# Twelve upper weight pieces and twelve value clips given to GpSimd in a quantised attention and expert kernel

## The chip, the core and the metric

The kernel runs on one core of a Trainium2 chip. The core has a matrix engine (TensorE, PE in the rows), VectorE (DVE), ScalarE (ACT), GpSimd (POOL), and a queue engine for transfers (SyncE, SP). They run side by side and wait for each other through semaphores. The metric is the device time of one launch in microseconds (us), as the median of several runs; less is better.

## The reference

A small vision block on 32 images of 36 tokens (1152 tokens, 192 features each):

```
h = patches @ proj_w.T + proj_b                       # 1152 x 768 -> 192
q, k, v = fq(layernorm(h)) @ fq(ww1).T                # 12 heads of 64
a = softmax(fq(q) @ fq(k).T / 8)                      # within one image
h = h + fq(fq(a) @ fq(v)) @ fq(ww2).T + bb2
n = layernorm(h); e = argmax(n @ Wg + bg)             # one of 4 experts per token
h = h + gelu(n @ W1[e] + b1[e]) @ W2[e] + b2[e]       # 192 -> 768 -> 192
```

fq(x) is s * (clip(round(x / s) + z, 0, 15) - z). The kernel keeps fq's integers: one instruction scales and rounds to int16, a second one clips to [-z, 15 - z] and writes bfloat16. "Clip" below means that second instruction, a maximum and a minimum from int16 to bfloat16.

## The kernel before, in words

Each engine has its own program, written out by hand; nothing is reordered later, so an instruction that waits holds up all that stands behind it on its engine.

The work has four stretches. First nine tiles of 128 tokens are embedded and normalised. Then come 15 steps, one for each pair of images (`for i in range(STEPS)` in every engine's program), in which four chunks of eight images are taken through the linear maps, the scores, the softmax and the product with the values, as a pipeline over the engines. After them the last tiles are normalised, the gate picks an expert for every token, and the tokens' rows are scattered to memory by expert. Last, twelve tiles of 128 slots go through the experts.

In a step, TensorE makes the scores of the next pair (L1151), the linear maps that are due (L1126 for the values, L1130 for queries and keys), the transposed probabilities (L1169) and the product with the values (L1186). ScalarE rounds the linear maps from PSUM to int16 (`vint` at L504 for the values, `kint` L510, `qint` L513), takes the exponential (L528), copies the transposed probabilities (L550) and rounds the outputs (L537). VectorE takes the maximum of each row of scores (L754), subtracts it (L760), sums the exponentials (L865), takes the reciprocal (L869), multiplies (L873) and clips (all clips are at L682, by the helper `clip`: `aq` probabilities, `q`, `k`, `v`, `oT` outputs). In some steps it also finishes a tile of tokens: the residual (L890), its moments (L692, L696), the variance plus epsilon (`veps`, L700) and, a step later, the normalised tile (`xn`, L905). Between the last two GpSimd takes the power -1/2 (`rstd`, L430, the helper `scale`). It also makes the low half of four tiles (L449).

Values come in groups of 768 columns, one for each pair of images: the tile `v` has seven buffers, `vint` two. `lin_groups(i)` says which groups step i holds; values of chunks 1 to 3 are due in steps 2, 3, 6, 7, 10 and 11, two in each. ScalarE makes `vint` in that step, VectorE clips it one step later.

The experts' float32 weights are brought in 16 pieces (`SPLITS`): eight of W1 with 768 columns, eight of W2 with 576. Each is split in two float16 parts: the upper part is the weight times 64, rounded to float16 (`split_high`, ScalarE L522), the lower part is what is left (`split_low`, VectorE L749, four in the steps and twelve behind the routing). `splits_at(i)` puts the eight upper parts of W1 into steps 1 to 8 and four of W2 into steps 11 and 12, at the end of a step of ScalarE; the last four come behind the steps.

GpSimd's program between the embedding and the scatter was nine short instructions, each of which waits for VectorE or ScalarE.

Of the kernel before, what the change touches and what calls it, by code (L numbers as in the profile page):

```python
# [11 lines left out]
ALU = mybir.AluOpType  # L12
# [10 lines left out]
WSCALE = 64.0  # L23
# [6 lines left out]
def vit_kernel(nc, patches_d, proj_w_d, proj_b_d, quant_d, ww1_d, ww2_d, bb2_d,  # L30
# [13 lines left out]
    _, NEXP, HM = b1_d.shape  # L44
# [23 lines left out]
    with ExitStack() as ctx:  # L68
# [3 lines left out]
        def sem(name):  # L72
            return ctx.enter_context(nc.semaphore(name))
# [126 lines left out]
        def xs(j):  # L200
# [35 lines left out]
        aT_ps, aT_ok, o_ps, o_int, o_ok = map(sem, ("aT_ps", "aT_ok", "o_ps", "o_int", "o_ok"))  # L236
        pr_ps, h2_ok, xn_ok, xhi_ok, xlo_ok, xnT_ps, xnT_ok, gate_ps = map(sem, (
            "pr_ps", "h2_ok", "xn_ok", "xhi_ok", "xlo_ok", "xnT_ps", "xnT_ok", "gate_ps"))
        pool_lo_ok = sem("pool_lo_ok")
        whi_ok, wlo_ok, route, onehot_ok, count_ps, logit_ok, slot_ok, slot_row_ok, expert_ok = map(sem, (  # L240
            "whi_ok", "wlo_ok", "route", "onehot_ok", "count_ps", "logit_ok", "slot_ok", "slot_row_ok", "expert_ok"))
        slotT_ps, slotT_ok, up_ps, g_ok, ghi_ok, glo_ok, down_ps, res_ok, y_ok = map(sem, (
# [52 lines left out]
        def splits_at(i):  # L295

            return [n for n in range(len(SPLITS)) if i == (n + 1 if n < EARLY else 11 + (n - EARLY) // 2 if n < EARLY + 4 else -1)]
# [75 lines left out]
        def _(pool):  # L373
# [54 lines left out]
            def scale(t):  # L428
                pool.wait_ge(var_ok, TT + t + 1)
                gp.tensor_tensor(rstd[:, t:t + 1], veps[:, t:t + 1], nhalf[:], ALU.pow).then_inc(rstd_ok, 1)  # L430
# [16 lines left out]
            def norm_low(t):  # L447
                pool.wait_ge(xhi_ok, 2 * t + 2)
                gp.tensor_tensor(row16[:, t, LO:LO + E], xn[:, t % 2], row16[:, t, HI:HI + E],  # L449
                                 ALU.subtract).then_inc(pool_lo_ok, 1)  # L450

            for t in range(6):
                scale(t)
                if 1 <= t <= POOL_LOWS:
                    norm_low(t - 1)
            scatter(0, 0, 1)
            scale(6)
            scatter(0, 1, 2)
# [16 lines left out]
        def _(act):  # L475
# [17 lines left out]
            def linear(x):  # L493
                kind, c, n = x
                j = lin_no[x]
                bank = lin_bank[j % 2]
                act.wait_ge(lin_ps, j + 1)
                if kind == "v":
                    p = c * PPC + n
                    if p == 0:  # L500
                        act.wait_ge(w_quant, 6)
                    if p >= 2:
                        act.wait_ge(v_ok, p - 1)
                    a.activation(vint[:, p % 2].rearrange("p (s n) -> p s n", s=2), bank[:, :, 0:INNER // 2],  # L504
                                 ACT.Copy, scale=rv).then_inc(lin_int, 1)
                    return
                if c >= 1 and n == 0:
                    act.wait_ge(q_ok if kind == "q" else k_ok, 2 * c if kind == "q" else c)
                if kind == "k":
                    a.activation(kint[:, 2 * n:2 * n + 2], bank[:, :, 0:CH], ACT.Copy, scale=rk).then_inc(lin_int, 1)  # L510
                    return

                a.activation(qint[:, :, :, n], bank[:, :, 0:CH].rearrange(  # L513
                                 "p g (i n) -> p g i n", n=NTOK), ACT.Copy, scale=rq).then_inc(lin_int, 1)

            def split_high(n):
                if n < EARLY:
                    act.wait_ge(w1_in[SPLITS[n][1]], 48)
                else:
                    act.wait_ge(w2_in[SPLITS[n][1]], 16)  # L520
                w, whi, _ = split_views(n)
                a.activation(whi, w, ACT.Copy, scale=WSCALE).then_inc(whi_ok, 1)  # L522

# [54 lines left out]
            for i in range(STEPS):  # L578
                exponential(i)
                if i == 0:  # L580
                    for x in lin_groups(-0.5):
                        linear(x)
                for x in lin_groups(i)[:1]:
                    linear(x)
                if 2 <= i < CHUNKS:
                    tokens_T(i)
                if i >= 2:
                    output(i - 2)
                for x in lin_groups(i)[1:]:
                    linear(x)  # L590
                if i < STEPS - 1:
                    for t in tiles_at(i, 2):
                        norm_high(t)
                if i >= 1:
                    probs_T(i - 1)
                for t in tiles_at(i, 3):
                    norm_T(t)
                for n in splits_at(i):
                    split_high(n)

            exponential(15)
            output(13)
# [46 lines left out]
        def _(dve):  # L649
# [31 lines left out]
            def clip(out, x, s, n=P, base=0):  # L681
                return d.tensor_scalar(out, x, lo[base:base + n, s:s + 1], hi[base:base + n, s:s + 1],  # L682
                                       ALU.max, ALU.min)
# [32 lines left out]
            def linear(x):  # L716

                kind, c, n = x
                dve.wait_ge(lin_int, lin_no[x] + 1)
                if kind == "q":  # L720

                    if c >= 2:
                        dve.wait_ge(s_ps, (c - 1) * PPC)
                    if c == 0:
                        dve.wait_ge(qpad_ok, 1)
                    for upper in range(2):
                        rows = slice(DH * upper, DH * upper + DH)
                        clip(q_slots[rows, c % 2, :, upper:upper + 11:5], qint[rows].rearrange("p g i t n -> p (g i) t n"),
                             QQ, DH, DH * upper).then_inc(q_ok, 1)
                elif kind == "k":  # L730
                    if c >= 2:
                        dve.wait_ge(s_ps, (c - 1) * PPC)
                    clip(k[:, c % 2], kint[:], KQ).then_inc(k_ok, 1)
                else:
                    p = c * PPC + n
                    if p >= VB:
                        dve.wait_ge(o_ps, p - VB + 1)
                    clip(v[:, p % VB], vint[:, p % 2], VQ).then_inc(v_ok, 1)

            def clips_of(i):  # L740

# [171 lines left out]
            for i in range(STEPS):  # L913
# [17 lines left out]
                        weights(n)  # L931
                for t in tiles_at(i, 1):
                    project(t)
                clipped = clips_of(i - 1) if i else []
                values = [x for x in clipped if x[0] == "v"]
                if old:
                    inverse(p)
# [151 lines left out]
        def _(pe):  # L1089
# [82 lines left out]

            def attend(p):
                pe.wait_ge(aT_ok, p + 1)
                pe.wait_ge(v_ok, p + 1)
                if p == 0:
                    pe.wait_ge(h_ok, TT)
                if p >= 1:
                    pe.wait_ge(o_int, p)

                for m in range(HB):
                    for hp in range(2):
                        for par in range(2):
                            rows = slice(64 * par, 64 * par + NTOK)
                            h = 2 * m + hp
                            last = mm(head_bank[DH * hp:DH * hp + DH, par, m * NTOK:(m + 1) * NTOK],  # L1186
                                      v[rows, p % VB, h * DH:(h + 1) * DH],
                                      aT[rows, p % 2, h * NTOK:(h + 1) * NTOK], start=True, stop=True)
                last.then_inc(o_ps, 1)
# [280 lines left out]
```

## Time and profile before

| | us |
|---|---|
| median of 3 runs | 173.92 (172.39 to 173.94) |
| the profiled execution, its own time | 171.95 |
| span of the trace, first to last instruction | 170.2 |
| TensorE busy | 137.1 (81%) |
| VectorE busy | 130.0 (76%) |
| ScalarE busy | 118.8 (70%) |
| GpSimd busy | 44.4 (26%) |

The table's shares are over the whole span. The steps lie from about 40 to 101 us of the span; what the change touches must be read from there. In a row of the trace the duration of an instruction overlaps the beginning of the next on the same engine, so the room that an instruction takes is better read from the start of one to the start of the next.

### The profile page before, as it was taken

How to read it: one execution, taken by the hardware profiler on the slowest of the kernel's cores; microseconds unless marked ns; L12 is line 12 of the kernel's file. 1: busy time of each engine (PE TensorE's matmuls, PEld its weight loads, DVE VectorE, ACT ScalarE, POOL GpSimd, SP SyncE). 2: the span in 40 equal slices, each digit the busy share in tenths (PEclk: the TensorE clock that was granted, in tenths of full speed). 3: DMA queues.
4: the chain of work that ended last, by engine and by line, in shares of the span. 5: the costliest groups of instructions: out<-in, count | busy, mean ns of one | idle time of the engine just before them, and what ended most of it. 6: DMA issues, size and time to landing. Idle time of an engine off the chain costs nothing.

```text
span 170.2 us, 5210 instructions
## 1 busy us (share of the span) xinstructions
PE 137.1 (81%) x1846; PEld 109.4 (64%) x1846; DVE 130.0 (76%) x391; ACT 118.8 (70%) x232; POOL 44.4 (26%) x108
## 2 busy tenths in 40 slices
PE   0499789998688969779977987715899999999960
PEld 0499577955455545546565765611389999999940
DVE  2626965999999999995999978669977676766750
ACT  8934457579899989998998746710277787777610
POOL 7212533341000022010112017864002222422242
PEclk9999999999999999995996557655799999999999
DMA  3799999999999999500000002342792100010000
GB/s 78 289 308 294 309 393 222 222 221 320 367 370 364 370 369 385 231 4 0 4 0 4 2 6 95 120 170 109 190 382 86 46 15 27 27 35 27 4 27 24
DMA packets 12922, 27.72 MB, mean 163 GB/s; under 512 B 1745, under 2 KB 8667, under 8 KB 12897
## 3 DMA queue, kind: packets, MB, share of 16 engines
q1 hardware_dynamic: 11744, 24.41, 45.5%
q0 software_dynamic: 1152, 2.97, 4.8%
q8 instruction: 16, 0.26, 0.6%
q14 instruction: 10, 0.07, 0.1%
HBM read 15.39 MB, written 12.29 MB: 163 GB/s over the span
## 4 chain that ended last, share of the span: by engine, by line
PE 38%; DVE 18%; issue 14%; ACT 13%; DMA 8%; SPq 4%; POOL 2%; POOLq 0%; ACTq 0%; DVEq 0%
PE lin_bank L1358 12%; DMA patches<-in_patches 8%; PE head_bank L1097 4%; PE head_bank L1370 3%; PE head_bank L1378 3%; PE head_bank L1371 3%; PE lin_bank L1391 3%; ACT vint L504 2%; ACT w L522 2%; PE lin_bank L1130 2%; ACT ex L528 2%; DVE row L890 2%; SPq L326 2%; PE lin_bank L1126 2%; DVE dif L760 2%
## 5 line engine op out<-in xcount | busy, mean ns | idle before, releaser
L643 ACT ACTIVATE q<-lin_bank,b 128x128 f32<-128x128 f32 x72 | 25.0, 369 | 7.4 <-PE lin_bank L1358 6.7
L1358 PE MATMUL lin_bank<-q,w 128*128 128x128 f16 x360 | 29.6, 219 | 0.5 <-ACT q L633 0.5
L1358 PEld LDWEIGHTS lin_bank<-q,w 128*128 x360 | 23.7, 98 | 0.9 <-issue 0.8
L1097 PE MATMUL head_bank<-proj_w,patches 128*128 128x192 f32 x84 | 17.8, 372 | 7.1 <-DMA patches<-in_patches 7.1
L1097 PEld LDWEIGHTS head_bank<-proj_w,patches 128*128 128x128 f32 x84 | 16.4, 222 | 7.4 <-issue 6.6
L430 POOL TENSOR_TENSOR rstd<-veps,nhalf 128x1 f32<-128x1 f32 x7 | 4.7, 667 | 55.7 <-DVE veps L700 55.7
L1370 PE MATMUL head_bank<-early,q 128*128 x72 | 17.7, 246 | 0.3 <-DVE q L1073 0.3
L1068 DVE CAST q<-q 128x384 f16<-128x384 f32 x24 | 8.6, 360 | 12.0 <-ACT q L643 12.0
L1378 PE MATMUL head_bank<-early,q 128*128 x72 | 17.7, 246 | 0.0
L1371 PE MATMUL head_bank<-early,q 128*128 x72 | 17.7, 246 | 0.0
L1130 PE MATMUL lin_bank<-xqT,ww1q 96*128 96x288 bf16 x96 | 15.4, 286 | 2.4 <-ACT kint L510 1.2
L504 ACT ACTIVATE vint<-lin_bank,fac 128x768 int16<-128x768 f32 x16 | 14.3, 903 | 2.7 <-PE lin_bank L1126 2.5
L1073 DVE TENSOR_TENSOR q<-q 128x384 f16<-128x384 f32 x24 | 13.3, 555 | 0.5
L1126 PE MATMUL lin_bank<-ww1q,xqT 96*128 96x384 bf16 x64 | 13.5, 338 | 0.0
L1151 PE MATMUL score_bank<-k,q 128*128 128x36 bf16 x256 | 9.2, 180 | 5.3 <-DVE dif L760 4.4
L1130 PEld LDWEIGHTS lin_bank<-xqT,ww1q 96*128 96x128 bf16 x96 | 8.5, 97 | 7.6 <-ACT kint L510 2.1
L1151 PEld LDWEIGHTS score_bank<-k,q 128*128 128x128 bf16 x256 | 7.9, 97 | 7.5 <-DVE dif L760 6.5
L423 POOL TENSOR_TENSOR rstd<-veps,nhalf 128x1 f32<-128x1 f32 x9 | 6.3, 705 | 21.4 <-DVE veps L700 21.4
L633 ACT COPY q<-score_bank 128x512 f16<-128x512 f16 x6 | 3.5, 585 | 11.7 <-PE score_bank L1334 11.7
L537 ACT ACTIVATE oint<-head_bank,fac 128x432 int16<-128x432 f32 x16 | 10.1, 633 | 2.0 <-PE head_bank L1186 2.0
L484 ACT ACTIVATE vint<-early,inv 96x768 int16<-96x768 f32 x6 | 5.5, 930 | 8.4 <-DVE ww1q L682 5.2
L467 POOL DMA_INDIRECT out<-q,v x5 | 4.9, 987 | 23.6 <-DVE q L1060 23.6
(158 smaller groups left out, 352.6 us busy)
## 6 DMA issues: line engine op xcount, KB each, us to landing
slots<-blank SPq DMA_DIRECT2D x3, 2938.0 KB, 22.3
patches<-in_patches SPq DMA_DIRECT2D x9, 384.0 KB, 11.8
early<-in_ww SPq DMA_DIRECT2D x3, 576.0 KB, 11.0
patches<-in_w SPq DMA_DIRECT2D x4, 384.0 KB, 11.6
patches<-in_w SPq DMA_DIRECT2D x8, 192.0 KB, 13.2
patches<-in_w SPq DMA_DIRECT2D x2, 576.0 KB, 12.9
v<-slots SPq DMA_DIRECT2D x5, 226.0 KB, 3.8
patches<-slots SPq DMA_DIRECT2D x4, 226.0 KB, 4.7
```

Of the source, the lines that this page charges most:

```text
L504: a.activation(vint[:, p % 2].rearrange("p (s n) -> p s n", s=2), bank[:, :, 0:INNER // 2], ACT.Copy, scale=rv).then_inc(lin_int, 1)
L537: a.activation(dst.rearrange("p m (r n) -> p r m n", r=2), head_bank[:, :, 0:HB * NTOK].rearrange("p r (m n) -> p r m n", m=HB), ACT.Copy, ...
L643: a.activation(g[:, j % 2, m], up_bank[n % 4][:, 0:P], ACT.Gelu, scale=1.0 / WSCALE, bias=b1[:, bass.ds(e, 1), m]).then_inc(g_ok, 1)
L1073: d.tensor_tensor(gs[:, j % 2, 1, ms], g[:, j % 2, ms], gs[:, j % 2, 0, ms], ALU.subtract).then_inc(glo_ok, 1)
L1097: last = mm(emb_bank[t][:, 0:E], patches[:, t, kc], proj_w[:, kc], start=kc == 0, stop=kc == KE - 1)
L1126: last = mm(bank[:, half, 0:INNER // 2], xqT[:, kc, 2 * p:2 * p + 2, :].rearrange("p i n -> p (i n)"), ww1q[:, kc, w0:w0 + INNER // 2], st ...
L1130: last = mm(bank[:, half, 0:CH], ww1q[:, kc, m * P:(m + 1) * P], xqT[:, kc, c * CI:(c + 1) * CI, 0:NTOK], start=kc == 0, stop=kc == 1)
L1151: last = mm(score_bank[:, s0:s0 + NTOK], q[:, c % 2, q0:q0 + P], k[:, c % 2, TRI * g + tri + x, cols], start=x == 0, stop=x == 1)
L1358: last = mm(up_bank[n % 4][:, 0:P], up_weights(j, part, m), xT[:, j % 3, piece], start=x == 0, stop=x == len(PASSES) - 1)
L1370: mm(down_bank[j % 2][:, 0:E], gs[:, j % 2, 0, m], we[:, 0:E], start=m == 0, stop=False)
L1371: mm(down_bank[j % 2][:, 0:E], gs[:, j % 2, 0, m], we[:, E:2 * E], start=False, stop=False)
L1378: last = mm(down_bank[j % 2][:, 0:E], gs[:, j % 2, 1, m], we[:, 0:E], start=False, stop=m == HM - 1)
```

## The change

GpSimd's program now has a loop over the 15 steps. In it stand the four low halves and the five powers as before, and new between them twelve upper weight pieces (L470, eight of 128x768 and four of 128x576) and twelve clips of values (L456, 128x768, for chunks 1 to 3). ScalarE keeps the last four upper pieces, VectorE keeps the clips of chunk 0. A semaphore `pool_v_ok` counts the new clips: ScalarE waits for it before it writes a buffer of `vint` again, TensorE before it uses the values. The arithmetic is the same.

```diff
+            def clip_values(p):
+                pool.wait_ge(lin_int, lin_no[("v", p // PPC, p % PPC)] + 1)
+                if p >= VB:
+                    pool.wait_ge(o_ps, p - VB + 1)
+                gp.tensor_scalar(v[:, p % VB], vint[:, p % 2], lo[:, VQ:VQ + 1], hi[:, VQ:VQ + 1],
+                                 ALU.max, ALU.min).then_inc(pool_v_ok, 1)
...
+            def split_high(n):
+                if n < EARLY:
+                    pool.wait_ge(w1_in[SPLITS[n][1]], 48)
+                else:
+                    pool.wait_ge(w2_in[SPLITS[n][1]], 16)
+                w, whi, _ = split_views(n)
+                gp.tensor_scalar(whi, w, WSCALE, None, ALU.mult).then_inc(whi_ok, 1)
+
+            for i in range(STEPS):
+                for t in tiles_at(i, 3):
+                    if t < POOL_LOWS:
+                        norm_low(t)
+                for n in splits_at(i):
+                    split_high(n)
+                for p in values_of(i)[:1]:
+                    clip_values(p)
+                for t in tiles_at(i, 1):
+                    scale(t)
+                for p in values_of(i)[1:]:
+                    clip_values(p)
+            scale(5)
@@ ScalarE @@
                     if p >= 2:
-                        act.wait_ge(v_ok, p - 1)
+                        if p - 2 < PPC:
+                            act.wait_ge(v_ok, p - 1)
+                        else:
+                            act.wait_ge(pool_v_ok, p - 1 - PPC)
...
             def split_high(n):
-                if n < EARLY:
-                    act.wait_ge(w1_in[SPLITS[n][1]], 48)
-                else:
-                    act.wait_ge(w2_in[SPLITS[n][1]], 16)
+                act.wait_ge(whi_ok, n)
+                act.wait_ge(w2_in[SPLITS[n][1]], 16)
...
-                for n in splits_at(i):
-                    split_high(n)
@@ VectorE @@
-                clipped = clips_of(i - 1) if i else []
+                clipped = [x for x in clips_of(i - 1) if x[0] != "v" or x[1] == 0] if i else []
@@ TensorE @@
-                pe.wait_ge(v_ok, p + 1)
+                if p < PPC:
+                    pe.wait_ge(v_ok, p + 1)
+                else:
+                    pe.wait_ge(pool_v_ok, p + 1 - PPC)
```

GpSimd's rows in the first steps and around step 7, as a piece of the difference (lines with a space are in both; the names ahead of a bracket are output and input, those in brackets the semaphores waited for):

```order
 L419 TENSOR_TENSOR row<-row,bb 128x192 [waits norm_ok] x2
-L430 TENSOR_TENSOR rstd<-veps,nhalf 128x1 [waits var_ok] x2
+L470 TENSOR_SCALAR w<-patches 128x768 [waits w1_in0,scales_ok]
+L470 TENSOR_SCALAR w<-patches 128x768 [waits w1_in0]
+L456 TENSOR_SCALAR v<-vint,lo,hi 128x768 [waits lin_int] x2
+L470 TENSOR_SCALAR w<-patches 128x768 [waits w1_in1]
+L456 TENSOR_SCALAR v<-vint,lo,hi 128x768 [waits lin_int]
+L456 TENSOR_SCALAR v<-vint,lo,hi 128x768 [waits o_ps,lin_int]
+L470 TENSOR_SCALAR w<-patches 128x768 [waits w1_in1]
+L470 TENSOR_SCALAR w<-patches 128x768 [waits w1_in2]
+L430 TENSOR_TENSOR rstd<-veps,nhalf 128x1 [waits var_ok]
```

```order
 L449 TENSOR_TENSOR row<-xn,row 128x192 [waits xhi_ok]
+L470 TENSOR_SCALAR w<-patches 128x768 [waits w1_in3]
+L456 TENSOR_SCALAR v<-vint,lo,hi 128x768 [waits o_ps,lin_int]
+L430 TENSOR_TENSOR rstd<-veps,nhalf 128x1 [waits var_ok]
+L456 TENSOR_SCALAR v<-vint,lo,hi 128x768 [waits o_ps,lin_int]
```

The powers now stand behind weight pieces and, in steps 7 and 11, behind a clip that waits for ScalarE.

VectorE's rows of step 12, before and then with the change (line numbers are 25 to 28 higher there):

```order
L869 RECIPROCAL rden<-den 108x8
L682 TENSOR_SCALAR oT<-oint,lo,hi 128x6x144
L682 TENSOR_SCALAR v<-vint,lo,hi 128x768
L873 SCALAR_TENSOR_TENSOR aint<-ex,inv,rden 108x288
L682 TENSOR_SCALAR v<-vint,lo,hi 128x768
L905 TENSOR_SCALAR xn<-row,mv,rstd 128x192
```

```order
L894 RECIPROCAL rden<-den 108x8
L710 TENSOR_SCALAR oT<-oint,lo,hi 128x6x144
L898 SCALAR_TENSOR_TENSOR aint<-ex,inv,rden 108x288
L930 TENSOR_SCALAR xn<-row,mv,rstd 128x192
```

The two clips of values have gone from between the others, and the normalised tile, which needs GpSimd's power, comes right behind the product.

## Rows read from the trace of the kernel before

**Rows 1.** The page, 40 slices: TensorE's granted clock in tenths of full speed.

```profile
PEclk9999999999999999995996557655799999999999
```

**Rows 2.** Stretches: length, then PE, PEld, DVE, ACT, POOL busy, clock, DMA.

```profile
40.00:101.00 61.00, 51.75 (x937) 34.48 (x936) 56.52 (x164) 55.20 (x105) 5.58 (x9) 0.89 0.53 188
101.00:117.00 16.00, 7.80 (x59) 6.12 (x58) 12.20 (x52) 6.86 (x18) 11.51 (x12) 0.61 0.31 117
```

**Rows 3.** The same for 13 steps, 43.0 to 93.6 us, summed.

```profile
sum 50.60, PE 42.00 PEld 27.45 DVE 47.21 ACT 47.29 POOL 5.58; mean PE 3.23 PEld 2.11 DVE 3.63 ACT 3.64 POOL 0.43
```

**Rows 4.** The chain that ended last: start, us, engine, tile, line.

```profile
53.19 0.74 ACT w L522
...
53.93 0.43 ACT ex L528
...
59.23 0.95 DVE w L749
```

**Rows 5.** Groups: count, busy us, mean ns of one, idle before.

```profile
L522 ACT ACTIVATE w<-patches 128x768 f16<-128x768 f32 x8 | 7.0, 878 | 0.0
L682 DVE TENSOR_SCALAR v<-vint,lo,hi 128x768 bf16<-128x768 int16 x16 | 7.5, 467 | 0.2 <-ACT vint L504 0.2
```

**Rows 6.** In order of time (start, us): two roundings of values on ScalarE.

```profile
47.69 0.90 ACT L504 ACTIVATE vint<-lin_bank,fac 128x768 int16<-128x768 f32 x1
...
50.05 0.91 ACT L504 ACTIVATE vint<-lin_bank,fac 128x768 int16<-128x768 f32 x1
```

**Rows 7.** VectorE in order of time, from 48.2 us and from 50.7 us.

```profile
48.22 0.43 DVE L682 TENSOR_SCALAR v<-vint,lo,hi 128x768 bf16<-128x768 int16 x1
48.56 0.51 DVE L873 SCALAR_TENSOR_TENSOR aint<-ex,inv,rden 108x288 int16<-108x288 f32 x1
...
50.76 0.46 DVE L754 TENSOR_REDUCE mx<-score_bank 108x8 f32<-108x288 f32 x1
...
52.09 0.45 DVE L682 TENSOR_SCALAR oT<-oint,lo,hi 128x864 bf16<-128x864 int16 x1
```

**Rows 8.** VectorE's wait for TensorE in step 10, in brackets.

```profile
80.96 0.46 DVE L754 TENSOR_REDUCE mx<-score_bank 108x8 f32<-108x288 f32 x1 [1.67 <-PE score_bank L1203]
```

**Rows 9.** GpSimd's groups, columns as in rows 5.

```profile
L449 POOL TENSOR_TENSOR row<-xn,row 128x192 f16<-128x192 f32 x4 | 2.2, 548 | 0.0
L392 POOL MEMSET blank<- 128x448 f32 x1 | 0.5, 471 | 0.1
L388 POOL CAST identh<-ident 128x128 f16<-128x128 f32 x1 | 0.3, 288 | 0.0
L407 POOL MEMSET earlier<- 128x1 f32 x1 | 0.1, 96 | 0.0
```

**Rows 10.** Two VectorE instructions with GpSimd at rest.

```profile
13.91 0.15 DVE L705 TENSOR_TENSOR rscale<-rstd,inv 128x1 f32<-128x1 f32 x1
...
14.71 0.33 DVE L682 TENSOR_SCALAR xq<-xint,lo,hi 128x192 bf16<-128x192 int16 x1
```

**Rows 11.** The same two beside a GpSimd instruction.

```profile
15.70 0.59 POOL L419 TENSOR_TENSOR row<-row,bb 128x192 f32<-128x192 f32 x1
15.86 0.44 DVE L705 TENSOR_TENSOR rscale<-rstd,inv 128x1 f32<-128x1 f32 x1
...
39.27 0.70 DVE L682 TENSOR_SCALAR xq<-xint,lo,hi 128x192 bf16<-128x192 int16 x1
39.31 0.59 POOL L419 TENSOR_TENSOR row<-row,bb 128x192 f32<-128x192 f32 x1 [1.87 <-DVE xint L709]
```

**Rows 12.** GpSimd's power beside VectorE's lower weight piece of 59.23 us.

```profile
59.28 1.32 POOL L430 TENSOR_TENSOR rstd<-veps,nhalf 128x1 f32<-128x1 f32 x1 [19.38 <-DVE veps L700]
```

**Rows 13.** Step 7 to 8: the power, ScalarE's third rounding, the normalised tile.

```profile
67.22 0.55 POOL L430 TENSOR_TENSOR rstd<-veps,nhalf 128x1 f32<-128x1 f32 x1 [6.62 <-DVE veps L700]
...
67.60 0.90 ACT L504 ACTIVATE vint<-lin_bank,fac 128x768 int16<-128x768 f32 x1
...
70.67 0.37 DVE L905 TENSOR_SCALAR xn<-row,mv,rstd 128x192 f32<-128x192 f32 x1
```

More of the change, by code:

```diff
@@ L238, in vit_kernel @@
             "pr_ps", "h2_ok", "xn_ok", "xhi_ok", "xlo_ok", "xnT_ps", "xnT_ok", "gate_ps"))
-        pool_lo_ok = sem("pool_lo_ok")
+        pool_lo_ok, pool_v_ok = map(sem, ("pool_lo_ok", "pool_v_ok"))
         whi_ok, wlo_ok, route, onehot_ok, count_ps, logit_ok, slot_ok, slot_row_ok, expert_ok = map(sem, (
@@ L450, in norm_low, with values_of @@
                                  ALU.subtract).then_inc(pool_lo_ok, 1)
[L452 to L455, printed above, removed]
+            def clip_values(p):
[4 more added lines that the diff above has]
+                                 ALU.max, ALU.min).then_inc(pool_v_ok, 1)
+            def values_of(i):
+                return [c * PPC + n for kind, c, n in lin_groups(i) if kind == "v" and c]
+            pool.wait_ge(scales_ok, 1)
+            def split_high(n):
[18 more added lines that the diff above has]
+            scale(5)
             scatter(0, 0, 1)
@@ L734, in linear @@
                 else:
[L735 to L738, printed above, removed]
+                    clip(v[:, n], vint[:, n % 2], VQ).then_inc(v_ok, 1)
             def clips_of(i):
```

## The prediction, as it was put on record before the changed kernel had run

> **What bounds the kernel now.** I read the page's slices first, then busy time by stretch, then the chain of waits over the steps, then each engine in order of time. Everything that the change touches lies in the 15 steps, from about 40 to 101 us; there both VectorE (56.5 of 61 us) and ScalarE (55.2) are nearly full, TensorE has 51.8 and GpSimd 5.6 [rows 2]. In the 13 full steps from 43.0 to 93.6 us, 50.6 us long, VectorE is busy 47.2 us, ScalarE 47.3, TensorE 42.0 [rows 3]. So neither engine alone sets the pace: the chain goes through ScalarE in some steps (the upper weight piece at 53.19 ends where the exponential begins) and through VectorE in others (59.23) [rows 4]. Taking work from one of them helps only until the other is the later one; the change takes work from both. The price is a third engine, which the trace shows getting in VectorE's way.
>
> **What the change removes.** ScalarE loses eight pieces of 768 columns and four of 576. A piece of 768 takes 0.88 us by its record [rows 5], but the next instruction begins 0.74 us after its start [rows 4], so 0.74 is its room; eight of them are 5.9 us, and four of 576 by their columns (0.74 x 576/768) 2.2: 8.1 us in all, of 47.3. ScalarE stops being the later engine anywhere in the steps. VectorE loses twelve of its sixteen clips of values, 0.467 us each by their records [rows 5]; the one at 48.22 has a record of 0.43 and a room of 0.34 up to 48.56 [rows 7], so I take 0.09 less than the mean record, about 0.37: 12 x 0.37 = 4.4 us. What VectorE waits in the 13 steps is 50.6 - 47.2 = 3.4 us [rows 3]. Of that 1.67 us is one wait for TensorE's scores and projection in step 10 [rows 8], which stays; the other 1.7 us come mostly from ScalarE and go. If nothing were added, VectorE would give back 4.4 + 1.7 = 6.1 us. TensorE idles 50.6 - 42.0 = 8.6 us in the same stretch [rows 3] and leaves room for it.
>
> **What GpSimd pays.** No row shows its TENSOR_SCALAR on 768 columns. The nearest is the CAST of 128 columns, 0.288 us: one tensor read, one written in another type. From below, each further column costs what it costs a MEMSET, (471 - 96)/447 = 0.84 ns: 0.288 + 640 x 0.00084 = 0.83 us. From above, all of the CAST but a MEMSET's 0.096 us is per column, 1.5 ns: 0.288 + 640 x 0.0015 = 1.25 us. Farther off, the subtraction with two inputs gives 2.35 ns a column, 1.9 us for 768 [rows 9]. Between the two near ends I take 1.0 us, and 0.8 for 576 columns. That is 20 x 1.0 + 4 x 0.8 = 23 us of new work on an engine with 45 us free in those steps; GpSimd itself is no bound. GPSIMD Engine Reference of the Trainium skill (section 3.1) puts the best case of an ordinary loop at about 1.8 cycles an element of a 1.2 GHz clock; by that a piece would be an estimated 1.15 us and a fixed part, the upper end, and the sum some 3 us worse.
>
> **What it costs VectorE.** This is the term that decides. A factor of one column takes VectorE 0.15 us, a clip of 192 columns 0.33 [rows 10]. When a GpSimd addition of 0.59 us begins beside them they take 0.44 and 0.70, and both end with GpSimd's instruction (16.30 against 16.29, 39.97 against 39.90) [rows 11]: they were held for 0.29 and 0.37 us, which is GpSimd's duration less 0.26 on the mean. It goes the other way too: a power that takes 0.55 us [rows 13] took 1.32 beside the lower weight piece that VectorE had begun just before [rows 12]. Not every VectorE instruction is of this kind. SBUF — State Buffer of the Trainium skill (section "Who interferes with whom") says that the two engines hold a shared port exclusively for a whole instruction, on VectorE's side for copies and scalar operations in a two-port mode and for instructions with two SBUF inputs; this trace agrees with the 0.29 and 0.37 us above. So in a step the clips, the product (L873), the normalised tile and the lower weight piece can be held. The two reductions, the subtraction from PSUM and the reciprocal can't; they stand together at the start of a step, from 50.76 to 52.09 us, 1.3 us [rows 7], and there a GpSimd instruction costs nothing.
>
> I set the 24 new instructions into VectorE's order at the time their inputs come. Clips follow ScalarE's rounding of values: the one that ends at 48.6 us [rows 6] meets VectorE's product at 48.56 [rows 7] and holds the clip of probabilities behind it; the one that ends at 50.96 falls into the free 1.3 us. Going so through all twelve, six meet a free stretch and six do not. Weight pieces follow the instruction before them; those that come while VectorE makes its own lower piece are held themselves and slide into the free stretch. I count five of twelve that hold VectorE. Eleven times 1.0 - 0.26 = 0.74 us is 8.1 us. The bounds are nothing, and all 24 at 1.25 - 0.26, 24 us. A gain from the hold is excluded: it only delays.
>
> **What else moves.** The power stands behind a clip that waits for ScalarE in steps 7 and 11. In step 7 the rounding ends at 67.60 + 0.90 = 68.50; clip 1.0, power 0.55: 70.05 us instead of 67.77. The normalised tile is due at 70.67 [rows 13], or at about 69.9 without the two clips ahead of it. I take it as hidden: ScalarE is earlier too by its missing pieces. Uncovered it costs up to 1 us in each of the two steps. The wait of ScalarE for GpSimd before it writes `vint` again looks two groups back, 2 us or more, and TensorE needs the values two steps or more after their clip; both cost nothing unless GpSimd falls a step behind. No DMA or queue is moved; the scatters come after the last new instruction. The last four pieces stay on ScalarE at their place, and their new wait is for pieces done 10 us before. Embedding, routing and experts keep their times.
>
> **The sum.** -4.4 - 1.7 + 8.1 = +2.0 us. The profiled execution took 171.95 us (span 170.2), 1.1% under the median of the three runs; it would become 173.9. The forecast stands against the median: 173.92 + 2.0 = 175.9 us.
>
> **The rivals.** (a) *The free stretches take nearly all of it*: a price of 0.83 us and four collisions of 0.57 make 2.3 us of holds against 6.1 given back: -3.8, 170.1 us. It decides below a mean hold of 6.1/24 = 0.25 us. For it speak the free 1.3 us in each step, and that GpSimd, held by VectorE's long pieces, is let go at the start of a free stretch; against it, the freed time is taken out of the held part of the step and not out of the free one. The same reference of the Trainium skill (section 4.1) calls GpSimd roughly line-rate on one input, which is the price of this case. (b) *An even account*: 0.83 us and eleven collisions, 6.3 - 6.1, about 174.1 us. (c) *The power comes late as well*: two times 1 us on top of the forecast, 177.9. (d) *1.25 us and fifteen collisions*: 15 us of holds, +8.8, 182.7 us. (e) *GpSimd at the rate of its two-input instruction*: 24 x about 1.8 us, 43 us beside its 6, as long as the steps themselves; it falls behind, and eleven holds of 1.6 us make +11.5, 185 us or more. (f) The change could fail to take load off the chain if TensorE were the pace; its 8.6 idle us speak against that, and it ends in (b). Over all lies TensorE's clock: it drops to half at about 77 us and from 91 us on [rows 1], and is 0.61 in the routing [rows 2]; a step that ends sooner or later may move that by a microsecond or two, either way.
>
> **How the numbers follow.** This kernel's runs differ by 0.9%, so less than 1% can't be told from no change. Forecast 0.33, (a) 0.22, (b) and (f) 0.28, (c) 0.07, (d) 0.07, (e) 0.03. The forecast's 175.9 lies 1.1% above; a quarter of its chance falls inside 1%. Case (b) spreads a little both ways. That gives faster by over 1% 0.23, within 1% 0.32, slower by over 1% 0.45. The range of 8 in 10 leaves out (e), most of (d) and the far half of (a): 170.5 to 180.5 us.
>
> **What would show it.** GpSimd's L456 and L470 at 0.8 to 1.3 us. ScalarE with some 10 us idle in the steps. VectorE's clip of probabilities and product with maxima near 1 us and ends that fall on GpSimd's; their sum over the medians is the hold, forecast 8 us. Steps of about the old length. I am wrong if these records hardly stretch, if GpSimd's take over 1.5 us, if VectorE idles before L905, or if the difference lies outside the steps.

## The result, and the profile after

The changed kernel takes 195.87 us (median of 4 runs, 194.47 to 196.43) where the kernel before takes 173.56 in the same comparison: ratio 1.129, 95% interval 1.120 to 1.137. It is 22.3 us slower. The forecast was 175.9 us with a range to 180.5, so the time lies far outside; of the rivals, (e), GpSimd falling behind, with a chance of 0.03 and "185 us or more", is the nearest to what came. The medians below are of all runs of a kernel, while the ratios leave out runs that came out in a slower state.

The page's first part and its chain by line, after the change:

```profile
PE 143.9 (74%) x1846; PEld 114.1 (59%) x1846; DVE 135.7 (70%) x379; ACT 112.7 (58%) x220; POOL 105.3 (54%) x132
```

```profile
POOL v L456 14%; PE lin_bank L1386 11%; DMA patches<-in_patches 7%; POOL w L470 7%; POOL early L470 3%; PE head_bank L1122 3%; PE head_bank L1398 3%; PE head_bank L1406 3%; PE head_bank L1399 3%; PE lin_bank L1253 2%; POOL rstd L430 2%; PE lin_bank L1151 2%; DMA slots<-row,slot 2%; PE lin_bank L1155 2%; SPq L326 1%
```

GpSimd, which stood on 2% of the chain before, is now its largest part inside the steps. The same chain by line, from 38 to 128 us alone:

```profile
by line: POOL v L456 31.0%; issue 25.9%; POOL w L470 14.6%; POOL early L470 7.2%; POOL rstd L430 3.8%; POOL row L449 2.9%; DVE q L710 2.8%; ACT vint L536 2.0%; ACT qint L545 1.5%; PE lin_bank L1151 1.4%; DVE row L915 0.9%; DVE stats L720 0.
```

The 13 steps from the maximum of step 2 to that of step 15 went from 50.6 us [rows 3] to 71.9. That is 21.3 of the 24.3 us by which the two profiled executions differ (spans of 194.5 and 170.2 us). Their busy times (length, then PE, PEld, DVE, ACT, POOL, clock, DMA share, GB/s):

```profile
44.50:116.40 71.90, 48.02 (x791) 31.25 (x791) 50.95 (x122) 40.50 (x76) 60.82 (x31) 0.77 0.39 138
```

ScalarE fell from 47.3 to 40.5 us, as the relief wanted, but GpSimd is busy 60.8 us, longer than the whole stretch had been. VectorE is busy 50.95 us instead of 47.21, so of the 21.3 us only 3.7 are longer work of VectorE and 17.6 are more waiting. TensorE's granted clock was 0.77 in these steps and 0.94 in the 13 steps before, and its matmuls took 48.0 us instead of 42.0. The chain hardly passes through TensorE (its largest line is 1.4%), so this is not the main term, but no run here sets its share apart. The groups (mean ns is the second number behind the bar) say why:

```profile
L456 POOL TENSOR_SCALAR v<-vint,lo,hi 128x768 bf16<-128x768 int16 x12 | 35.8, 2991 | 10.3 <-ACT vint L536 10.3
L470 POOL TENSOR_SCALAR w<-patches 128x768 f16<-128x768 f32 x8 | 17.5, 2190 | 0.0
L470 POOL TENSOR_SCALAR early<-proj_w 128x576 f16<-128x576 f32 x2 | 3.3, 1654 | 0.0
```

A clip takes 2.99 us, a W1 piece 2.19, a W2 piece 1.65; the prediction had taken 1.0, 1.0 and 0.8. The 24 instructions are 59.9 us of work (35.8 + 17.5 + 4 x 1.65), not 23. VectorE's waits over the steps (who waited for whom: us in total, times, longest):

```profile
DVE xn L930 <- POOL rstd L430: 13.2, 2, 7.7
DVE w L774 <- POOL w L470: 3.4, 2, 2.7
DVE oT L710 <- ACT oint L567: 2.1, 3, 0.9
```

The waits for a power are those of the normalised tiles of steps 8 and 12, whose powers stand behind a clip of GpSimd; these two steps lengthened by 6.2 and 8.6 us. Steps 4 to 6, in which VectorE waited for weight pieces, lengthened by 7.7 us together; the others became 1.2 us shorter in sum. In order of time around the power of step 12, GpSimd and then VectorE:

```profile
101.66 3.28 POOL L470 TENSOR_SCALAR early<-proj_w 128x576 f16<-128x576 f32 x2
104.92 2.93 POOL L456 TENSOR_SCALAR v<-vint,lo,hi 128x768 bf16<-128x768 int16 x1
107.82 0.57 POOL L430 TENSOR_TENSOR rstd<-veps,nhalf 128x1 f32<-128x1 f32 x1
108.39 2.92 POOL L456 TENSOR_SCALAR v<-vint,lo,hi 128x768 bf16<-128x768 int16 x1
```

```profile
97.66 0.15 DVE L728 TENSOR_SCALAR veps<-mv 128x1 f32<-128x1 f32 x1
...
100.22 0.51 DVE L898 SCALAR_TENSOR_TENSOR aint<-ex,inv,rden 108x288 int16<-108x288 f32 x1
108.42 1.05 DVE L930 TENSOR_SCALAR xn<-row,mv,rstd 128x192 f32<-128x192 f32 x1 [7.69 <-POOL rstd L430]
109.40 0.34 DVE L710 TENSOR_SCALAR aq<-aint,lo,hi 108x288 bf16<-108x288 int16 x1
```

The variance was ready at 97.8 us. GpSimd came to its power ten microseconds later, behind work that ran through without a gap. Before, it took the power at once [rows 13]. And the tile at 108.42 took 1.05 us instead of 0.37, because the next clip had begun at 108.39: that is the hold of [rows 11].

### The profile page after: what moved, and what is told of

Its sections match the earlier page's. It is cut to its first block, busy times and chain, and to the rows that moved or that the text cites. A ratio compares the mean times of both kernels' runs of the same rounds, so it can differ in the third digit from the quotient of the medians.

```text
span 194.5 us, 5215 instructions
## 1 busy us (share of the span) xinstructions
PE 143.9 (74%) x1846; PEld 114.1 (59%) x1846; DVE 135.7 (70%) x379; ACT 112.7 (58%) x220; POOL 105.3 (54%) x132
## 4 chain that ended last, share of the span: by engine, by line
PE 33%; POOL 29%; issue 14%; DMA 10%; DVE 5%; SPq 4%; ACT 4%; POOLq 0%; ACTq 0%; DVEq 0%
POOL v L456 14%; PE lin_bank L1386 11%; DMA patches<-in_patches 7%; POOL w L470 7%; POOL early L470 3%; PE head_bank L1122 3%; PE head_bank L1398 3%; PE head_bank L1406 3%; PE head_bank L1399 3%; PE lin_bank L1253 2%; POOL rstd L430 2%; PE lin_bank L1151 2%; DMA slots<-row,slot 2%; PE lin_bank L1155 2%; SPq L326 1%
## 5 line engine op out<-in xcount | busy, mean ns | idle before, releaser
L456 POOL TENSOR_SCALAR v<-vint,lo,hi 128x768 bf16<-128x768 int16 x12 | 35.8, 2991 | 10.3 <-ACT vint L536 10.3
L1122 PE MATMUL head_bank<-proj_w,patches 128*128 128x192 f32 x84 | 17.6, 370 | 7.4 <-DMA patches<-in_patches 7.4
L1122 PEld LDWEIGHTS head_bank<-proj_w,patches 128*128 128x128 f32 x84 | 16.3, 220 | 7.7 <-issue 6.6
L496 POOL DMA_INDIRECT out<-q,v x5 | 5.7, 1135 | 23.5 <-DVE q L1085 23.5
L423 POOL TENSOR_TENSOR rstd<-veps,nhalf 128x1 f32<-128x1 f32 x9 | 6.4, 706 | 21.2 <-DVE veps L728 21.2
L1155 PE MATMUL lin_bank<-xqT,ww1q 96*128 96x288 bf16 x96 | 16.6, 305 | 1.6 <-ACT vint L536 0.9
L470 POOL TENSOR_SCALAR w<-patches 128x768 f16<-128x768 f32 x8 | 17.5, 2190 | 0.0
L1093 DVE CAST q<-q 128x384 f16<-128x384 f32 x24 | 9.2, 383 | 11.3 <-ACT q L671 10.7
L1194 PE MATMUL probT_bank<-identb,aq 108*36 108x108 bf16 x128 | 7.2, 247 | 11.4 <-DVE aq L710 11.3
L930 DVE TENSOR_SCALAR xn<-row,mv,rstd 128x192 f32<-128x192 f32 x9 | 5.2, 582 | 14.2 <-POOL rstd L430 13.2
L1151 PE MATMUL lin_bank<-ww1q,xqT 96*128 96x384 bf16 x64 | 15.0, 366 | 0.0
L558 ACT ACTIVATE ex<-dif,fac 108x288 f32<-108x288 f32 x16 | 8.7, 542 | 9.4 <-DVE dif L785 9.4
```

The source lines that it names most:

```text
L456: gp.tensor_scalar(v[:, p % VB], vint[:, p % 2], lo[:, VQ:VQ + 1], hi[:, VQ:VQ + 1], ALU.max, ALU.min).then_inc(pool_v_ok, 1)
L470: gp.tensor_scalar(whi, w, WSCALE, None, ALU.mult).then_inc(whi_ok, 1)
L1122: last = mm(emb_bank[t][:, 0:E], patches[:, t, kc], proj_w[:, kc], start=kc == 0, stop=kc == KE - 1)
L1151: last = mm(bank[:, half, 0:INNER // 2], xqT[:, kc, 2 * p:2 * p + 2, :].rearrange("p i n -> p (i n)"), ww1q[:, kc, w0:w0 + INNER // 2], st ...
L1155: last = mm(bank[:, half, 0:CH], ww1q[:, kc, m * P:(m + 1) * P], xqT[:, kc, c * CI:(c + 1) * CI, 0:NTOK], start=kc == 0, stop=kc == 1)
```

## The experiments

Theory A is that the time is GpSimd's own: its instructions are dear, it becomes the bound, and what stands behind them on its queue comes late. Theory B is that VectorE is held by GpSimd's instructions. The kernel before, as run beside the experiments, took 173.70 to 173.89 us.

**e1, the pieces alone.** The clips go back to VectorE.

```diff
-                for p in values_of(i)[:1]:
-                    clip_values(p)
                 for t in tiles_at(i, 1):
                     scale(t)
-                for p in values_of(i)[1:]:
-                    clip_values(p)
...
```

> The twelve upper weight pieces stay on GpSimd, the twelve clips go back to VectorE (the order of GpSimd: low half, pieces, power). Theory A, GpSimd's own time and the powers queued behind it: the pieces are 8 x 2.19 + 4 x 1.65 = 24 us, which fit into 61 us of steps, and no power stands behind a clip; so nearly all of the +22 us goes: 173 to 177 us. Theory B, the holds of VectorE by GpSimd instructions: half of the 24 instructions are left, so about half of the slowdown should be left: 183 to 186 us.

Measured: 176.87 us, ratio 1.021 (1.012 to 1.030). It is at the upper end of theory A's range, far under B's.

**e2, the clips alone.** The pieces go back to ScalarE.

```diff
-                for n in splits_at(i):
-                    split_high(n)
                 for p in values_of(i)[:1]:
                     clip_values(p)
...
```

> The twelve clips stay on GpSimd, the pieces go back to ScalarE. Theory A: 12 x 2.99 = 36 us of clips; two clips of 3 us in each of steps 2, 3, 6, 7, 10, 11 are longer than what is left of a step, and a power stands between them in steps 7 and 11, so GpSimd is late there but catches up in between: 180 to 188 us. Theory B: 183 to 186 us, as for the pieces alone. The two together separate the theories by the difference between the two runs: A wants at least 6 us, B none.

Measured: 184.22 us, ratio 1.060 (1.051 to 1.068), 7.4 us above e1, for the same number of instructions. The time alone lies in both theories' ranges; the difference from e1 speaks for A, which wanted at least 6 us where B wanted none. VectorE waited 7.7 us for two powers:

```profile
DVE xn L932 <- POOL rstd L430: 7.7, 2, 4.4
```

The parts alone cost 3.0 and 10.4 us, together 13.4; both at once 22.3. The 9 us between are as theory A has it, for an engine that is filled beyond the length of the steps only by both; the difference alone does not prove it.

**e3, the power first.** Both parts, but another order in GpSimd's step.

```diff
+                for t in tiles_at(i, 1):
+                    scale(t)
                 for n in splits_at(i):
                     split_high(n)
-                for p in values_of(i)[:1]:
-                    clip_values(p)
-                for t in tiles_at(i, 1):
-                    scale(t)
-                for p in values_of(i)[1:]:
+                for p in values_of(i):
                     clip_values(p)
```

> As the changed kernel, but in each step of GpSimd the power comes ahead of the pieces and clips (after the low half). In the changed kernel VectorE waited 13.2 us for two powers. Theory A in its narrow form (it is the place of the power in the queue): 13 us come back, 183 us. Theory A in its wide form (GpSimd has 60 us of new work in steps that took 61 us, whatever the order): a power ahead of a clip now waits for VectorE and holds the clips behind, little comes back, 190 to 197 us. Theory B: no change, 195.9 us.

Measured: 190.79 us, ratio 1.099 (1.092 to 1.106): 5 us come back, the other 17 stay. GpSimd in the 13 steps, now 67.1 us long:

```profile
44.30:111.40 67.10, 44.96 (x784) 29.31 (x791) 50.80 (x122) 40.55 (x76) 61.12 (x31) 0.82 0.42 148
```

It is still busy 61.1 us. Steps 8 and 12 fell from 10.4 and 11.9 us to 5.2 and 5.0, but steps 10 and 14 grew from 3.6 and 2.8 to 7.8 and 7.6, because the powers that they wait for now stood behind work left over from earlier steps:

```profile
DVE xn L928 <- POOL rstd L430: 9.2, 3, 4.9
```

The place of the power is a cost of its own, but the smaller one. Most of the waiting only moved, as theory A has it for an engine with more work than the steps have room for.

**e4, the relief without its price.** The eight W1 pieces and the twelve clips are left out, and zeros stand in their place; the four W2 pieces of the steps stay on ScalarE.

```diff
+            gp.memset(w1[:].rearrange("p e s n -> p (e s n)").bitcast(F32), 0.0).then_inc(whi_ok, EARLY)
+            gp.memset(v[:].rearrange("p b n -> p (b n)").bitcast(F32), 0.0).then_inc(pool_v_ok, 1)
...
-                for n in splits_at(i):
-                    split_high(n)
-                for p in values_of(i)[:1]:
-                    clip_values(p)
...
```

> Left out: the eight upper pieces of W1 (the tile is set to zero once, in GpSimd's idle time at the start) and the twelve clips of chunks 1 to 3 (v set to zero likewise); the four W2 pieces of the steps are made by ScalarE as before. It is what the change takes off ScalarE (5.9 us) and VectorE (4.4 us) with no price on GpSimd. The prediction's terms give -4.4 - 1.7 = -6 us, about 167.5 us. If TensorE was closer to the pace than I took it, -1 to -3 us, 171 us.

Measured: 170.73 us, ratio 0.985 (0.976 to 0.993), 3.1 us faster. The 13 steps take

```profile
43.40:89.60 46.20, 39.26 (x786) 27.04 (x791) 43.38 (x121) 41.86 (x82) 5.85 (x9) 0.97 0.59 214
```

4.4 us less than in [rows 3]. From the maximum of step 15 to the first expert matmul the stretch was longer than before, 31.4 against 29.4 us, and lost 2.0 of it; why is open. So the relief was worth some 3 us (the interval allows 1 to 4), and a lower price on GpSimd would hardly have made the change worth more, but for the 2.2 us (by the prediction) of W2 pieces that this run leaves on ScalarE. The prediction's 6.1 was about twice what came. Nearly half of the 4.4 us lies between the maxima of steps 10 and 11, before and in this run (columns as above):

```profile
75.64:80.96 5.32, 4.49 (x54) 2.83 (x56) 3.44 (x11) 4.68 (x9) 1.06 (x2) 0.68 0.00 0
73.95:77.14 3.19, 3.09 (x65) 2.29 (x65) 3.19 (x10) 3.19 (x8) 0.56 (x1) 1.00 0.00 0
```

TensorE's granted clock there was 0.68 before and 1.00 in this run. It is the place where VectorE had waited 1.67 us for TensorE [rows 8], and here that wait is gone. In e12 below, with nothing left out, the same stretch took 3.19 us at 1.00, in e11, with all pieces on ScalarE, 5.05 us at 0.72. What sets the clock there is not shown.

**e5, the clip's bounds as constants.**

```diff
-                gp.tensor_scalar(v[:, p % VB], vint[:, p % 2], lo[:, VQ:VQ + 1], hi[:, VQ:VQ + 1],
+                gp.tensor_scalar(v[:, p % VB], vint[:, p % 2], -8.0, 7.0,
```

> As the changed kernel, but GpSimd's clips take their bounds as constants (-8 and 7, the same values) and not from two columns of a tile. The clips took 2.99 us, the pieces, with one operation and a constant, 2.19. If the bounds' form is what makes a clip dearer, clips fall to about 2.2 us, 12 x 0.8 = 9 us less on GpSimd, and about half of it comes back, as GpSimd sets the end of the steps only in part of them: 186 to 191 us. If it is the second operation, nothing changes: 195.9 us. Theory B (holds): no change of the time in either case.

Measured: 196.3 us, ratio 1.134 (1.123 to 1.144), no change from the 195.9, as forecast for the case that the form of the bounds is not the cause. The clips:

```profile
L456 POOL TENSOR_SCALAR v<-vint 128x768 bf16<-128x768 int16 x12 | 34.1, 2845 | 10.7 <-ACT vint L536 10.0
```

2.85 us instead of 2.99: the form of the bounds is not what makes them dear.

**e6 and e9, nearer to what the prediction had assumed.** The same 24 instructions, twenty of them narrower, with the rest of their columns left out. e6 keeps the order; e9 has the order of e3 on top.

```diff
-                gp.tensor_scalar(v[:, p % VB], vint[:, p % 2], lo[:, VQ:VQ + 1], hi[:, VQ:VQ + 1],
+                gp.tensor_scalar(v[:, p % VB, 0:256], vint[:, p % 2, 0:256], lo[:, VQ:VQ + 1], hi[:, VQ:VQ + 1],
...
+                if n < EARLY:
+                    w, whi = w[:, 0:336], whi[:, 0:336]
```

> As the changed kernel, with its 24 instructions in the same places and with the same waits, but narrower, so that they cost about the 1 us that the prediction took: clips 256 of 768 columns, the eight pieces of W1 336 of 768 (the rest of both left out, the tiles set to zero once in GpSimd's idle time at the start), the four pieces of W2 whole. If the price was the only step that failed, the sum of the prediction holds: 175.9 us, or with the relief as measured (-3 us) and 8 us of holds 178 to 179. If the holds are worth less than 8 us, 172 to 175. If the number of instructions and their place in the queue matter and not their price, 185 us or more.

> The kernel with 24 narrow instructions (clips 256 of 768 columns, W1 pieces 336, the rest left out), and the power ahead of pieces and clips in each step. With the power behind a clip it took 178.4 us, and VectorE waited 5.2 us for two powers, though each GpSimd instruction was only 1.1 to 1.4 us. If the place in the queue is a cost of its own, apart from the price: those 5 us go, 172.5 to 174.5 us. If the time sits in the holds of VectorE: 177 to 178.5.

Measured: e6 178.43 us, its four runs widely spread; the ratio, 1.018 (1.002 to 1.034), counts two of them, 175.80 and 177.34 us, and not the profiled one, 179.51. e9 175.19 us, ratio 1.008 (1.005 to 1.011). Of e6:

```profile
L459 POOL TENSOR_SCALAR v<-vint,lo,hi 128x256 bf16<-128x256 int16 x12 | 16.3, 1360 | 17.0 <-ACT vint L542 17.0
L476 POOL TENSOR_SCALAR w<-patches 128x336 f16<-128x336 f32 x8 | 8.6, 1076 | 0.0
```

```profile
DVE xn L938 <- POOL rstd L433: 5.2, 2, 3.7
```

The 24 instructions are 31.7 us of work here (16.3 + 8.6, and 6.8 for the four W2 pieces), against 59.9 in the changed kernel and 23 in the prediction. By the ratio e6 is 3.1 us slower than the kernel before, so some 19 of the 22.3 us are gone. VectorE still waits 5.2 us for powers in e6's profiled run and 2.8 in e9's. That this costs time at the low price is not shown: the two intervals overlap. e9 came out 0.7 us above the 172.5 to 174.5 that I had put down for it.

**e7, clips that nobody waits for.** In the kernel before, from 39.9 us on, into a tile of its own.

```diff
...
+            for x in range(6):
+                step(gp.tensor_scalar(dump[0:EC], ww1q[:, 0, 0:INNER], lo[0:EC, VQ:VQ + 1], hi[0:EC, VQ:VQ + 1],
+                                      ALU.max, ALU.min))
```

> The kernel before, and GpSimd makes six more clips of 96x768 into a tile that nobody reads, from about 39.9 us on, when it would idle until 59.3 us; nobody waits for them, so only a hold of VectorE can cost time. If VectorE is held for a whole GpSimd instruction (2.9 us), its clips and products in steps 1 to 4 come to a stop for most of 17 us: +8 us or more, 182. If it is held only in the first microsecond or less, as the rows of the changed kernel look, six times up to 0.7 us: +1.5 to +4 us, 175.5 to 178. If holds cost nothing: 173.8.

Measured: 176.48 us, ratio 1.015 (1.010 to 1.021), +2.6 us for 20.9 us of GpSimd work: 0.4 us a clip, inside the 175.5 to 178 put down for short holds. The hold is not for the whole instruction. In GpSimd's row the six run as one; VectorE in the same time:

```profile
39.86 20.88 POOL L456 TENSOR_SCALAR dump<-ww1q,lo,hi 96x768 bf16<-96x768 bf16 x6
```

```profile
40.32 0.86 DVE L688 TENSOR_SCALAR v<-vint,lo,hi 128x768 bf16<-128x768 int16 x1
41.10 0.51 DVE L879 SCALAR_TENSOR_TENSOR aint<-ex,inv,rden 108x288 int16<-108x288 f32 x1
41.64 0.35 DVE L688 TENSOR_SCALAR aq<-aint,lo,hi 108x288 bf16<-108x288 int16 x1
```

The clip that follows GpSimd's start stretches from 0.43 to 0.86 us; the product and the next clip run undisturbed while the same GpSimd instruction goes on. But the beginning is not the only place. The fifth of the six, and VectorE beside it:

```profile
53.96 3.10 POOL L456 TENSOR_SCALAR dump<-ww1q,lo,hi 96x768 bf16<-96x768 bf16 x1
```

```profile
54.36 0.81 DVE L688 TENSOR_SCALAR oT<-oint,lo,hi 128x864 bf16<-128x864 int16 x1
55.09 0.47 DVE L688 TENSOR_SCALAR v<-vint,lo,hi 128x768 bf16<-128x768 int16 x1
...
56.30 0.84 DVE L688 TENSOR_SCALAR aq<-aint,lo,hi 108x288 bf16<-108x288 int16 x1
```

The clip at 54.36 is held near GpSimd's beginning. The one at 56.30 takes 0.84 us instead of 0.35 and ends at 57.14, just after GpSimd's 57.06. What begins between the two runs at its usual length.

**e10, a price list.** Eight forms in GpSimd's idle time, the kernel before otherwise.

```diff
...
+            step(gp.tensor_copy(dump[0:EC], ww1q[:, 0, 0:INNER]))
+            step(gp.tensor_copy(dump[:, 0:448], src))
+            step(gp.tensor_scalar(dump[0:EC], ww1q[:, 0, 0:INNER], 1.0, None, ALU.mult))
+            step(gp.tensor_scalar(dump[:, 0:448], src, 1.0, None, ALU.mult))
+            step(gp.tensor_scalar(dump[0:EC], ww1q[:, 0, 0:INNER], -8.0, 7.0, ALU.max, ALU.min))
+            step(gp.tensor_scalar(dump[:, 0:448], src, -8.0, 7.0, ALU.max, ALU.min))
...
```

> The kernel before, and in GpSimd's idle time from 39.9 us eight instructions into an unused tile, one form each: copy and one multiplication and two bounds, from bfloat16 (768 columns) and from float32 (448 columns), and the last two at 128 columns. If a second operation is what makes a clip dearer than a piece, two bounds cost some 30% more per column than one multiplication for either type; if it is the type, the bfloat16 rows stand out for one operation too. The copy should show what misled the forecast: 1.5 ns a column or less, against 2.6 for the multiplication.

One run, 177.55 us. The rows:

```profile
40.10 0.82 POOL L456 COPY dump<-ww1q 96x768 bf16<-96x768 bf16 x1
40.99 0.56 POOL L457 CAST dump<-blank 128x448 bf16<-128x448 f32 x1
41.64 2.22 POOL L458 TENSOR_SCALAR dump<-ww1q 96x768 bf16<-96x768 bf16 x1
43.94 1.67 POOL L459 TENSOR_SCALAR dump<-blank 128x448 bf16<-128x448 f32 x1
45.69 3.43 POOL L460 TENSOR_SCALAR dump<-ww1q 96x768 bf16<-96x768 bf16 x1
49.21 1.72 POOL L461 TENSOR_SCALAR dump<-blank 128x448 bf16<-128x448 f32 x1
51.01 0.54 POOL L462 TENSOR_SCALAR dump<-blank 128x128 bf16<-128x128 f32 x1
51.63 0.64 POOL L463 TENSOR_SCALAR dump<-blank 128x128 bf16<-128x128 f32 x1
```

A copy of 768 columns takes 0.82 us, which is the lower bound that the prediction had worked out from the CAST of 128, 0.83. A TENSOR_SCALAR with one multiplication takes 2.22 for the same columns. A second operation costs 1.2 us more from bfloat16 and next to nothing from float32 (1.72 against 1.67), so neither "the operation" nor "the type" alone, as I had set them against each other, says it. The two sources also differ in partitions and columns, and the one-operation rows multiply where the others compare; what makes the difference is open. Each row is one instruction beside VectorE's work: the same W1 piece took 2.19 us on the mean in the changed kernel and 2.43 in e1.

**e11, fills that nobody waits for.** GpSimd only writes.

```diff
...
+            for x in range(22):
+                step(gp.memset(dump[:], 0.0))
```

> The kernel before, and GpSimd fills an unused tile of 128x768 with zeros 22 times from 39.9 us on (0.74 us each), with nobody waiting. Six idle clips of the same total length cost 2.6 us. If VectorE is held by GpSimd's reading of its input, fills hold nothing: 173.9 us, and VectorE's clips keep their 0.35 us. If GpSimd's writing holds it too, VectorE's clips stretch and the time rises by 1 us or more.

Measured: 178.2 us, ratio 1.026 (1.023 to 1.030; two runs). Reading is not needed for a hold. VectorE's groups over 39 to 125 us (mean ns; undisturbed they are 508 and 350):

```profile
L878 DVE SCALAR_TENSOR_TENSOR aint<-ex,inv,rden 108x288 int16<-108x288 f32 x16 | 8.1, 508 | 0.1
L687 DVE TENSOR_SCALAR aq<-aint,lo,hi 108x288 bf16<-108x288 int16 x16 | 6.6, 414 | 0.2
```

The clips stretch, the product with its two inputs does not; in the changed kernel, where GpSimd reads, it does (616 ns). Both agree with what SBUF — State Buffer of the Trainium skill (section "Who interferes with whom") says of the two kinds; that the pair is kept for the whole instruction, e7 does not bear out.

**e8 and e12, a candidate.** Pieces 0 to 4 stay on ScalarE, pieces 5 to 11 go to GpSimd behind the powers, all clips on VectorE; e12 is the same kernel with more runs.

```diff
...
                 for t in tiles_at(i, 1):
                     scale(t)
+                for n in splits_at(i):
+                    if n >= 5:
+                        split_high(n)
...
```

> A candidate. Pieces 0 to 4 on ScalarE as before, pieces 5 to 11 on GpSimd, behind the powers; all clips on VectorE. With all twelve pieces on GpSimd, steps 2 to 5 took 2.4 us more than before (five pieces back to back there) and the later steps the same as before. So 173.5 to 174.5 us if that is additive; below 173 if the holds in the late steps are fewer with the power first.

> The candidate once more, for a tighter interval: pieces 5 to 11 on GpSimd behind the powers, all else as before. The first time it took 172.98 against 173.89 us, ratio 0.9971 with an interval that holds 1. If it is a gain, 0.993 to 0.998; if not, an interval around 1.000.

Measured: e8 172.98 us, ratio 0.997 (0.992 to 1.003); e12 171.94 us, ratio 0.993 (0.989 to 0.997). The second interval is clear of 1: 0.7% faster, at the edge of the 0.993 to 0.998 put down for a gain; the first one leaves it open. The profiles do not show the gain: e12's span is 170.2 us, as long as that of the kernel before, and the 2.1 us won between the maxima of steps 10 and 11 are lost elsewhere. It is the only version here that does all of the work and is not slower than the kernel before.

## Why the prediction was wrong, point by point

**What GpSimd pays: the step that failed.** "Between the two near ends I take 1.0 us." Both ends came from a CAST and a MEMSET, and the changed instructions are TENSOR_SCALAR. GpSimd's CAST grows from 0.29 us at 128 columns to 0.56 at 448 (e10), some 0.85 ns a column; its TENSOR_SCALAR grows by 2.6 (the piece, from e6's 336 to 768 columns: (2190 - 1076)/432) to 3.2 (the clip, (2991 - 1360)/512). The one row that was near, the two-input subtraction with 1.9 us for 768 columns [rows 9], I had put aside as farther off, and it too was under the 2.19 and 2.99 measured. So "GpSimd itself is no bound" fell: 60 us of work for steps of 50.6. e6 confirms that this term is most of the miss: with 31.7 us of work in the same places the kernel is 3.1 us slower than the one before, where the forecast had 2.0. Rival (e) had GpSimd fall behind, but took its 11.5 us from holds alone; in the changed kernel most of the loss is VectorE waiting.

**The power behind the clip: a second step, smaller.** "I take it as hidden." It cost 13.2 us of waiting at the real price, and 5.2 in e6's profiled run. The wait itself needed no high price: the clip ahead of the power waits for ScalarE's rounding, and the power's input is ready by then. In e6 the clip ended and the power began at 75.19 us, 1.5 us too late for VectorE. Putting the power first gave 5 us at the full price; at the low one no gain is shown. Rival (c) had named it at 2 us.

**The relief: right in kind, too large.** 6.1 us forecast, 4.4 in the steps and 3.1 in the whole (e4). In e4's 13 steps VectorE's work fell by 3.8 us, near the 4.4 forecast, but its waiting only by 0.6, from 3.4 to 2.8, where the prediction had 1.7. The wait of 1.67 us for TensorE, which was to stay, was gone (0.4 us of another was left); the waits for ScalarE, which were to go, were 1.1 us before and 1.5 in e4.

**The holds: the sum was right, its parts were not.** Forecast 8.1 us from eleven of 0.74. VectorE's groups from 39 to 125 us, before and then in the changed kernel:

```profile
L873 DVE SCALAR_TENSOR_TENSOR aint<-ex,inv,rden 108x288 int16<-108x288 f32 x16 | 8.1, 508 | 0.1
L682 DVE TENSOR_SCALAR q<-qint,lo,hi 64x1728 bf16<-64x1728 int16 x6 | 4.3, 722 | 0.1
L682 DVE TENSOR_SCALAR oT<-oint,lo,hi 128x864 bf16<-128x864 int16 x8 | 3.8, 478 | 0.6 <-ACT oint L537 0.6
```

```profile
L898 DVE SCALAR_TENSOR_TENSOR aint<-ex,inv,rden 108x288 int16<-108x288 f32 x16 | 9.9, 616 | 0.1
L710 DVE TENSOR_SCALAR q<-qint,lo,hi 64x1728 bf16<-64x1728 int16 x6 | 6.6, 1095 | 0.1
L710 DVE TENSOR_SCALAR oT<-oint,lo,hi 128x864 bf16<-128x864 int16 x8 | 5.2, 648 | 2.1 <-ACT oint L567 2.1
```

That is 16 x 0.11 + 6 x 0.37 + 8 x 0.17 = 5.3 us, and with the probabilities' clips (0.9), the normalised tiles (1.8), the two lower pieces (0.6) and one weight clip (0.6) 9.3 us. That it comes near 8.1 is luck: these are holds by instructions of 2.2 to 3.0 us, for which the prediction's rule gives 1.9 to 2.7 us each. With instructions of 1.1 to 1.7 us (e6) the same groups stretch by 1.8 us in all. "GpSimd's duration less 0.26" does not scale: e7 shows 0.4 us for a clip of 3.5.

**Nothing outside the steps** was to move, and little did: of the 24.3 us between the two traces 1.5 lie between the last maximum and the experts' first matmul (30.8 against 29.4 us). Another 1.5 lie just ahead of the 13 steps, where the first two weight pieces meet VectorE: its clips between 39.7 and 44.5 us took 1.6 us longer than before.

## What to carry to other kernels

Price an instruction that moves to GpSimd by a row of the same operation, not by one that moves as many bytes: in e10 a multiplication or a clip took 2.7 to 4.2 times as long as the copy or cast of the same columns. Then set the sum of the moved work against the length of the stretch, and look at the short instructions that already live on that queue: each new one ahead of them, above all one that itself waits, becomes part of their latency. Work without a consumer nearby, placed behind the short ones, can cost nothing, as the candidate shows, while its gain is bounded by what is gained when the work is simply left out; that run is worth making first.

## What the runs showed of the hardware that I had not expected

- GpSimd's TENSOR_SCALAR on 768 columns of 96 partitions took 2.22 us with one operation and 3.43 with two from bfloat16; the copy took 0.82. From float32 (448 columns) the second operation added 0.05 us (1.67 and 1.72).
- A GpSimd TENSOR_SCALAR of 3 to 4 us held VectorE's clips near its beginning and near its end, and not between: in the changed kernel the tile that began with it at 108.42 us ended at 109.47, and the next clip, at 109.40, took its usual 0.34 while GpSimd went on until 111.31; in e7 the clip of 56.30 us was held to GpSimd's end. The two-input product was held near a beginning alone, 1.07 us at 55.16 us in the changed kernel. Why these two places is open; the ends are those of GpSimd's records.
- GpSimd fills held VectorE's clips as well, and 22 of them cost the kernel 4.5 us, but never its two-input product (508 ns before and beside them).
